# Layer 0's router and experts in one block, with GpSimd taking two of four groups' low parts

## The reference

```python
def _route(x, gate_w, gate_bias):            # 64 experts in 8 groups of 8
    scores = sigmoid(x @ gate_w.T)
    choice = scores + gate_bias
    # a group's score: its two best choices, summed; the best 4 groups are kept
    # of these the best 8 experts; their scores, divided by their sum, times 2.5
    ...
def _mlp(x, gw, uw, dw):
    return silu(x @ gw.T) * (x @ uw.T) @ dw.T  # inner width 88 for each expert
out = sum over experts of rw[:, e] * _mlp(x, Wg[e], Wu[e], Wd[e]) + _mlp(x, Sg, Su, Sd)
x = layernorm(x + out)                         # before it and after it: attention and layernorm
```

## Time and profile before

| | |
|---|---|
| median of 3 runs | 1407.01 us (1405.93 to 1410.32) |
| profiled execution | 1402.02 us, its span 1400.3 us |
| busy over the span | PE 91%, DVE 80%, ACT 64%, POOL 34% |
| mean granted clock of PE | 0.946 of full speed |

### The profile page before, as it was taken

The page is one execution under the profiler, slowest core; times in us unless marked ns, Lnnn a source line. Parts: engine busy times, 40 slices in busy tenths (PEclk is TensorE's granted clock), DMA queues, the critical chain, the costliest instruction groups (busy, mean ns, idle before and its releaser), DMA issues. The chain is left out here.

```text
span 1400.3 us, 21389 instructions
## 1 busy us (share of the span) xinstructions
PE 1279.3 (91%) x7374; PEld 711.9 (51%) x7374; DVE 1114.2 (80%) x1726; ACT 898.5 (64%) x1503; POOL 481.3 (34%) x988
## 2 busy tenths in 40 slices
PE   5898987169999999999889999999999998999998
PEld 2222224157777777777643232223222337777776
DVE  5677763758999999999758788888889747688886
ACT  4988873034555555555453788888888866767775
POOL 4565551014334343334142244224422422221210
PEclk8898988579999999999999999999999999999999
DMA  5422200064666666666236555434342201121200
GB/s 156 127 56 66 63 21 7 0 134 110 147 143 154 148 151 151 147 146 152 79 113 146 111 156 133 121 102 104 88 123 61 53 11 52 62 91 46 91 31 31
DMA packets 70020, 135.87 MB, mean 97 GB/s; under 512 B 13031, under 2 KB 44328, under 8 KB 63112
## 3 DMA queue, kind: packets, MB, share of 16 engines
q1 hardware_dynamic: 68760, 133.46, 37.5%
q10 hardware_dynamic: 1152, 1.05, 0.2%
HBM read 116.87 MB, written 16.29 MB: 95 GB/s over the span
## 5 line engine op out<-in xcount | busy, mean ns | idle before, releaser
L1589 ACT ACTIVATE a_PR<-n1a_C 128x512 f32<-128x512 f32 x576 | 299.6, 603 | 79.5 <-PE n1a_C L1495 79.4
L1604 DVE CUSTOM_DVE_ANT_0 OC_last<-a_mring,a_COR 128x1024 bf16<-128x1024 f32 x256 | 302.6, 1218 | 42.4 <-PE a_mring L1462 42.1
L1432 POOL TENSOR_SCALAR_AFFINE_SELECT a_PR<-a_PR 128x128 f32<-128x128 f32 x512 | 136.2, 296 | 250.2 <-ACT a_PR L1589 249.7
L868 ACT ACTIVATE e_HH<-e_H 128x512 fp32r<-128x512 f32 x184 | 116.4, 633 | 158.3 <-DVE e_H L916 157.5
L1495 PE MATMUL n1a_C<-a_QP,a_KP 74*128 74x512 bf16 (+3 forms) x768 | 176.1, 332 | 4.4 <-ACT a_PR L1589 3.5
L402 ACT ACTIVATE a_PR<-a_ring,a_ng 128x1024 f32<-128x1024 f32 (+1 forms) x160 | 150.2, 1045 | 26.0 <-PE a_ring L345 26.0
L427 DVE TENSOR_SCALAR a_PR<-a_PR,a_lo,a_hi 128x1024 f32<-128x1024 f32 (+1 forms) x160 | 119.2, 763 | 56.1 <-ACT a_PR L402 55.6
L1514 PE MATMUL n1a_C<-a_PR,a_V 128*9 128x512 f32 (+3 forms) x1536 | 152.1, 492 | 0.0
L887 DVE TENSOR_TENSOR e_HL<-e_H,e_HH 128x512 fp32r<-128x512 f32 x138 | 139.4, 1010 | 13.5 <-DVE e_H L904 0.5
L810 POOL TENSOR_TENSOR e_HL<-e_H,e_HH 128x512 fp32r<-128x512 f32 x46 | 78.5, 1706 | 180.5 <-ACT e_HH L868 180.5
L1883 DVE TENSOR_TENSOR e_HL<-e_GL,e_HH 128x512 fp32r<-128x512 f32 x144 | 109.5, 765 | 38.3 <-ACT e_HH L1851 34.7
(11 more groups left out here) (257 smaller groups left out, 2252.6 us busy)
## 6 DMA issues: line engine op xcount, KB each, us to landing
e_ROUTE<-routing SPq DMA_DIRECT2D x24, 704.0 KB
a_QP<-q_parts SPq DMA_DIRECT2D x72, 192.0 KB
e_RAW<-in_w_chunks SPq DMA_DIRECT2D x46, 192.0 KB, 7.4
a_QM<-q_parts SPq DMA_DIRECT2D x64, 128.0 KB, 2.8
e_GATE<-gates SPq DMA_DIRECT2D x8, 1024.0 KB, 4.4
e_ROUTE<-routing SPq DMA_DIRECT2D x8, 640.0 KB
a_KP<-k_parts SPq DMA_DIRECT2D x24, 192.0 KB
e_ROUTE<-routing SPq DMA_DIRECT2D x8, 576.0 KB
```

What stands on the lines that cost most here:

```text
L868: nc.scalar.activation(HH[n % NH][:], HT[n % NH][:], ACT.Copy).then_inc(high_done, 1)
L1432: last = nc.gpsimd.affine_select(out=d, in_=d, compare_op=keep, fill=0.0, base=0, pattern=[[step, P]], channel_multiplier=-step)
L1589: nc.scalar.activation(PR[:, g % NPR, j, :], ring[n % NRING][:], ACT.Exp).then_inc(s_read, 1)
L1604: nc.vector.tensor_tensor_reduce(out=junk[:, i % 2, :], in0=mring[k % 2][:], in1=COR[:, c:c + S], scale=1.0, scalar=-3.0e38, op0=ALU.mult, ...
```

## The change

`route_l0` and `experts_l0` become one block, `moe_l0`, and some of its work is done in the normalisation before it.

- In `normalise` ("n0a"): SP loads the router's weights and four chunks of expert weights; PE makes the logits of a group as soon as it is rescaled; ACT makes the high part of X and the scores; POOL makes both parts of three chunks' weights and the low part of X.
- In `moe_l0` DVE's routing instructions have the first 20 products of silu and up between them. The choice of the two best experts of a group is made with maxima and minima of halves. Hidden values of 24 steps are kept (`NTR`). The multiplication by the routing weight is 20 steps behind the product, the low part 21, the down product 23.
- The shared expert's down product is one float32 product with the weights in `RAW`, with no split.
- POOL makes the low part of every odd step, and the high part of the weights, six chunks ahead of the low parts that follow it. From chunk 8 on the weights' low part is on DVE. ACT copies the transposed routing weights.
- Weights have 8 buffers and 4 for the raw values, routing rows three as before.
- In `project_l1` the sixteen matmuls at the end become five, and five are added in front of the last but one group's product.

```diff
-def normalise(nc, name, X, consts, signals, turn, Y=None, update=None, C=None, out=None, load_ahead=None):
+def normalise(nc, name, X, consts, signals, turn, Y=None, update=None, C=None, out=None, load_ahead=None, ahead=None):
...
                     variance_of(g)
                     spread_inverse(g - 1)
+                    if ahead is not None and g >= 2:
+                        ahead.logits_of(pe, g - 2, done, base + g - 1, C[g - 2])
                 spread_inverse(NG - 1)
+                if ahead is not None:
+                    for g in range(NG - 2, NG):
+                        ahead.logits_of(pe, g, done, base + g + 1, C[g])
...
+                if ahead is not None:
+                    for g in range(NG - 2, NG):
+                        ahead.high_of_x(act, g, done, base + g + 1)
+                    for g in range(NG):
+                        ahead.scores_of(act, g, C[g])
+            if ahead is not None:
+                @block.gpsimd
+                def _(pool):
+                    for c in range(ahead.FIRST):
+                        ahead.split(pool, c)
+                    for g in range(NG):
+                        ahead.low_of_x(pool, g)
...
+    def load_chunk(self, sp, c):
+        if c >= NRAW:
+            self.await_low(sp, c - NRAW)
+        if NRAW <= c < NRAW + CHS:
+            sp.wait_ge(self.down_done, (c - NRAW + 1) * NG)
+        sp.dma_start(self.RAW[c % NRAW][:], self.a["w_chunks"][c]).then_inc(self.w_loaded[c % NRAW], 16)
+    def split(self, pool, c):
+        raw, high, low = self.RAW[c % NRAW], self.WH[c % NSLOT], self.WL[c % NSLOT]
+        pool.wait_ge(self.w_loaded[c % NRAW], (c // NRAW + 1) * 16)
+        if c >= NSLOT:
+            pool.wait_ge(self.down_done, (c - NSLOT + 1) * NG)
+        self.nc.gpsimd.tensor_copy(high[:], raw[:]).then_inc(self.w_high, 1)
+        if c < NSLOT:
+            pool.wait_ge(self.w_high, c + 1)
+            self.nc.gpsimd.tensor_tensor(low[:], raw[:], high[:].bitcast(F32), ALU.subtract).then_inc(self.w_low_pool, 1)
+    def split_low(self, dve, c):
+        raw, high, low = self.RAW[c % NRAW], self.WH[c % NSLOT], self.WL[c % NSLOT]
+        dve.wait_ge(self.w_high, c + 1)
+        self.nc.vector.tensor_tensor(low[:], raw[:], high[:].bitcast(F32), ALU.subtract).then_inc(self.w_low_dve, 1)
...
+            def _(sp):
+                for c in range(NRAW, 2 * NRAW):
+                    ahead.load_chunk(sp, c)
+                for g in range(NG):
+                    sp.wait_ge(kept, g + 1)
+                    sp.dma_start(routing[:, grp(g)], RT[:, grp(g)]).then_inc(stored, 16)
+                sp.wait_ge(stored, 16 * NG)
+                for c in range(CHS, CHS + NR):
+                    load_route(c)
+                for c in range(2 * NRAW, NCH):
+                    ahead.load_chunk(sp, c)
+                    if c - 2 * NRAW - 1 >= CHS + NR:
+                        load_route(c - 2 * NRAW - 1)
+                for c in range(NCH - 2 * NRAW - 1, NCH):
+                    load_route(c)
...
+            def _(pool):
+                for c in range(ahead.FIRST, NCH + POOL_BEHIND):
+                    if c < NCH:
+                        ahead.split(pool, c)
+                    if c - POOL_BEHIND >= CHS:
+                        for n in range((c - POOL_BEHIND) * NG, (c - POOL_BEHIND + 1) * NG):
+                            if on_pool(n):
+                                low(n)
...
+            def _(pe):
+                for n in range(N):
+                    if n == TURN:
+                        turn_weights()
...
+                    product(psG[n % 2], s, 0, g).then_inc(gate_ready, 1)
+                    product(psU[n % 2], s, 1, g).then_inc(up_ready, 1)
+                    if 3 <= n < NSH + 3:
+                        down_shared(n - 3)
+                    if n - DOWN >= NSH:
+                        down(n - DOWN)
...
+            def _(act):
+                for n in range(N + BEHIND + 1):
+                    if n == TURN:
+                        for g in range(NG):
+                            act.wait_ge(turned, g + 1)
+                            nc.scalar.activation(RT[:, grp(g)], banks[g][0:NE0, :], ACT.Copy).then_inc(kept, 1)
+                    if n < N:
+                        silu(n)
+                    if n - BEHIND - 1 >= NSH:
+                        high(n - BEHIND - 1)
...
+                for n in range(BEHIND + NSH, N + BEHIND + 1):
+                    if n < N:
+                        product(n)
+                    if n % NG == 0 and n // NG + 1 < NCH:
+                        ahead.split_low(dve, n // NG + 1)
+                    if n - BEHIND - 1 >= NSH:
+                        low(n - BEHIND - 1)
+                    if n - BEHIND < N:
+                        weigh(n - BEHIND)
...
-                        pe.wait_ge(cor_loaded, 32)
...
+                    if g == NG - 2:
+                        pe.wait_ge(cor_loaded, 32)
+                        keep_busy(psV, 5)
...
-                keep_busy(psQ[0], 16)
+                keep_busy(psQ[0], 5)
```

More of the change, by code:

```diff
@@ L727, in experts_l0, with moe_l0 @@
+def moe_l0(nc, X, Y, last_outputs, ahead, consts, routing, part):
+    NR = 3
     NH = 4
-    LAG = 3
+    TURN = 20
+    BEHIND = 20
+    DOWN = BEHIND + 3
+    NTR = 24
     NSH = CHS * NG
@@ new lines, in link @@
+                def link(ins, then=0):
+                    links[0] += 1
+                    ins.then_inc(step, 1)
+                    for _ in range(then):
+                        product(products[0])
+                        products[0] += 1
+                    dve.wait_ge(step, links[0])
+                by_group = ch.rearrange("p t (g e) -> p (t g) e", g=NGRP)
+                flat = lambda t: t[:].rearrange("p t g -> p (t g)")
+                wide = lambda t, k: flat(t).unsqueeze(2).to_broadcast([P, NT_TOK * NGRP, k])
@@ new lines, in _ @@
+                link(v.tensor_tensor(best[:], best[:], second[:], ALU.add), 1)
+                others = best[:].unsqueeze(2).to_broadcast([P, NT_TOK, NGRP, NGRP])
+                own = best[:].unsqueeze(3).to_broadcast([P, NT_TOK, NGRP, NGRP])
+                pair = t1.rearrange("p t (i j) -> p t i j", i=NGRP)
+                link(v.tensor_tensor(pair, others, own, ALU.is_ge), 1)
+                link(v.tensor_tensor(t1, t1, ahead.tri[:, 0:NGRP].rearrange("p i j -> p (i j)").unsqueeze(1)
+                                     .to_broadcast([P, NT_TOK, NE0]), ALU.mult), 1)
@@ new lines, in _ @@
+                for n in range(products[0], BEHIND + NSH):
+                    product(n)
+                for n in range(BEHIND + NSH, N + BEHIND + 1):
+                    if n < N:
+                        product(n)
+                    if n % NG == 0 and n // NG + 1 < NCH:
[4 more added lines that the diff above has]
+                        weigh(n - BEHIND)
@@ L1997, in build @@
         with ExitStack() as part:
-            Y = sbuf(nc, part)("Y_m0", [P, TOK], F32)
-            route_l0(nc, X, a["gate_w"], a["gate_bias"], a["earlier"], consts, routing0)
-            experts_l0(nc, X, Y, routing0, a["w_chunks"])
+            ahead0 = AheadMoeL0(nc, part, X, a)
+            normalise(nc, "n0a", X, consts, signals, 0, update=output0, load_ahead=ahead0.load, ahead=ahead0)
+            moe_l0(nc, X, OC, last, ahead0, consts, routing0, part)
             def load_ahead(sp):
```

396 lines of the change are left out of this document (179 added, 217 removed).

## The result

| | median | runs | against before |
|---|---|---|---|
| before | 1407.8 us | 4 runs, 1405.9 to 1410.3 | |
| after | 1429.28 us | 4 runs, 1424.8 to 1438.3 | 1.0159, 95% interval 1.0106 to 1.0213 |

The account below looks back on a forecast made before the run. It took PE and DVE as both near their limits, DVE with POOL slightly behind PE. The stage came to 465.4 us in place of 448.8, +16.6; with -2.0 for the projection, net +14.6 on 1407.0: 1421.6 us, range 1395 to 1441.

Parts of the forecast that it names:

- step 5: 38 steady chunks: DVE waits about 2.0 us for POOL's cast behind a low part; 9.22 us a chunk against 8.37, 350.4 together.
- step 2: Routing with 20 products between: DVE's list 38 us, PE hidden; with transposes and PE's next step, product 20 starts at 43.4.
- step 4: Behind product 28: DVE stands 15 us for chunk 8's weights, whose load SP issues behind seven DMAs of routing rows.
- The normalisation: Block before the experts: grows by 5.0 us through the last group's logits, high part, table load, sigmoids and X's low part.
- Steps 20 to 27: After routing: these steps are on PE, 8 x 1.36 = 10.9 us, so product 28 comes at 54.3.
- the first rival: Steady chunks: routing rows, not the cast, hold DVE; no chunk below 8.4 us; 1390.4 us in all; chance 0.14.
- The end: Behind the last products: 21 low parts and multiplications left, two steps 3.2 us, 37.3 us to the last matmuls.
- Layer 1's projection: Block behind the experts: with five matmuls at its end PE ends earlier and ACT is last: -2.0 us.
- That chunk 8 would not wait: Second rival, at chunk 8: weights pass the routing rows, so 15 us less, 1406.3 us, no change; chance 0.08.
- The clock fell: Rival: PE's clock falls, more likely only in the routing part and at chunk starts, +13 and +10: 1445 us; chance 0.10.
- DVE and POOL shut each other out: Expert chunks and end: instructions reading two SBUF tiles exclude each other; side by side would make 18 us less.

Follow-up runs that it names:

- raw_first: Changed kernel with the loads of the weights of chunks 8 to 11 issued before the store of the routing weights: 1419.94 us, ratio 1.0078.
- rows_early: Changed kernel with each chunk's routing rows issued in front of the weights' load that stood before them in SP's list: 1424.5 us, ratio 1.0140.
- proj_old: Changed kernel with layer 1's projection as before (sixteen matmuls at its end, none in front of the last but one group's product): 1432.37 us, ratio 1.0168.
- behind7: Changed kernel with POOL's cast of a chunk's weights one chunk's low parts further ahead (POOL_BEHIND 7 in place of 6): 1395.82 us, ratio 0.9918.
- three pairs: Kernels with new against old layer 1 projection, otherwise alike: the changed kernel, the kernel before, and a later faster candidate; -1, -1 and -5 us for the new one.
- combined: Changed kernel with the edits of behind7, raw_first and rows_early together: 1381.21 us, ratio 0.9800.
- pool_first: Changed kernel with only one of four low parts on POOL, that of step 4k + 1, POOL_BEHIND still 6: 1400.37 us, ratio 0.9932.

## Why the prediction was right, step by step

The sign, the place and the mechanism were right; the time was 7.7 us short, within the range. The stage took +24.4 where +16.6 was added up, so the shortfall lies in the stage, most of it in step 5. Two smaller errors went opposite ways (+3.3 in step 2, -1.5 in step 4) and partly cancelled.

1. *The normalisation*: +5.0 forecast, 244.86 - 240.44 = +4.4. Of this 0.8 had arisen before the normalisation (its first ACT instruction stands at 222.67, before at 221.88), so the block itself grew by 3.6.
2. *Routing and 20 products*: product 20 forecast at 43.4 after the block's start, measured 46.7. DVE's list was through at 40.5 (38 forecast), and product 20 came 6.2 later (5.4 forecast): PE made its matmuls at a granted clock of 0.54, in 2.7 us. The small instructions together took about 2.0 less than the sum, since one starts before the last has ended. What the sum lacked: one of the three reductions reads with a stride and took 2.11, not 1.23; the first two instructions were held up by POOL's subtraction (0.26 and 0.70); and DVE did wait for PE, four times, 2.5 us in all. The forecast held PE hidden at 1.36 for a step. In these steps it also does a down product of the shared expert (L850), and the clock is 1.00. DVE's product and PE in order of time:

```profile
262.97 0.69 DVE L924 TENSOR_TENSOR e_T<-e_SG,e_psU 128x512 f32<-128x512 f32 x1 [1.03 <-PE e_psU L835]
...
265.22 0.69 DVE L924 TENSOR_TENSOR e_T<-e_SG,e_psU 128x512 f32<-128x512 f32 x1 [0.43 <-PE e_psU L835]
```

```profile
258.26 1.02 PE L850 MATMUL e_acc<-e_T,e_RAW 128*128 128x512 f32 x2
258.72 0.80 PE L833 MATMUL e_psG<-e_XH,e_WH 128*128 128x512 f32 x1
259.36 0.40 PE L834 MATMUL e_psG<-e_XL,e_WH 128*128 128x512 f32 x1
...
260.50 1.02 PE L850 MATMUL e_acc<-e_T,e_RAW 128*128 128x512 f32 x2
```

   A step is 2.24 us so, and DVE asks for one each 1.9. The float32 product takes 0.87 (1.10 from its start to the second matmul behind it, less 0.23 for the first), more than the 0.68 (half of 1.36) of three fp32r matmuls. The forecast said in passing that these down products shrink by 2 us together; they grow, by 0.19 each, and in these steps it is what makes DVE wait.
3. *Steps 20 to 27*: 10.9 forecast, 10.9 measured (291.54 to 302.44).
4. *The new wait*: 15 forecast, 13.5 measured, at the place and by the load that were named. raw_first shows that its cause is the order in SP's list. DVE went on at 71.8, forecast 70.1.
5. *38 chunks*: 9.22 forecast, 9.16 to 9.2 by the cast alone (the chunk above, rows_early), 9.42 in fact. DVE's wait is 1.9 (2.03 forecast), PE's idle 0.7. The term that the forecast lacked is the mechanism of the first rival, which I had weighed only as an alternative: rows come late even at 9.2 a chunk, since their issue stands behind a load that waits. Over 37 distances this 0.2 is 7.4 us, nearly all of what the block took beyond the forecast (468.8 against 460.4); in `proj_old` it was about half of that. The order inside a chunk was as forecast too: the low part that POOL's other one shuts out ended 8.6 after the chunk's first product.
6. *The end*: 37.3 forecast, 36.5 measured, two steps 3.16 (3.2 forecast).
7. *Layer 1's projection*: -2.0 forecast; the block itself is 3.2 shorter (32.7 in place of 35.9), but in the profiled execution the attention behind it had a granted clock of 0.79 over its first 70 us, not 0.95, and took 14 us longer. By the three pairs what is left is -1 to -5, none of it beyond what a pair can tell, so this term is neither borne out nor refuted.

The +24.4 is of one execution and the +22 of the medians. They fit together if most of the 11.8 us behind the experts belong to that execution more than to the kernel; this isn't shown by itself, but the same code took between 659.9 and 672.7 us there in nine kernels, and 672.7 is this one.

On the rivals: the routing rows do not set the cycle, but add to it. The first rival's floor, no chunk below 8.4, does not hold either: behind7 has 8.34 and `combined` 8.26. That chunk 8 would not wait was wrong by 13.5 us (and its time, by the forecast's own 15 us, should read 1406.6, not 1406.3). The clock fell in three places, but not in the steady chunks (1.00 there): at the transposes (0.55 from 284 to 289), while PE stood at chunk 8 and for its first matmuls behind that (0.50 from 312 to 322), and in the attention. At chunk 8 it cost nothing that shows, since the first chunk behind it took 9.15 us, no more than the others.

DVE and POOL shut each other out as forecast: DVE's low part takes 0.69 alone and 1.25 beside POOL's. The Trainium skill ("SBUF — State Buffer", section "SBUF: two separate sides") calls this an exclusive lock, and the trace agrees. No run takes the lock away alone, so its price isn't measured. But it did not make the move a loss: behind7 has POOL's two low parts and the lock and is 0.8% faster than the kernel before, and both its chunk and its end are shorter than those of pool_first, with half as many low parts on POOL. From 0.69 to 1.25 in each of some ten pairs at the end is about 6 us by estimate, which is where it still weighs.

## What to carry over

When work moves to another engine, write down that engine's list and ask of each instruction that somebody else waits for (here a cast of 0.5 us) what stands in front of it and what that waits for; its place may cost more than the work moved: here it was worth 34 us of 1429. The same goes for the engine that issues DMAs: a small load needed soon (192 KB here) does not belong behind 3 MB needed later; that was worth 11 us. A distance that a pipeline needs at its start is paid at its end, in time in which the engine that sets the pace has little to do, unless it shrinks on the way.

## What the runs showed of the hardware

- One float32 product of 128x512 from weights of 128x128 took 0.87 us of PE at full clock, three fp32r matmuls of that shape 0.68, both read from the distances between starts (the rows at step 2 above).
- A reduction of 128x1024 elements by eights took 1.21 us reading in order and 2.11 us where its inner index had a stride of eight elements:

```profile
L982 DVE TENSOR_REDUCE r_below<-OC 128x128 f32<-128x1024 f32 x1 | 2.1, 2114 | 0.0
...
L981 DVE TENSOR_REDUCE r_ranks<-OC 128x128 f32<-128x1024 f32 x1 | 1.2, 1212 | 0.0
```

- The same stretch of code gets different clocks on PE. With the new projection, in the profiles of nine kernels that differ only in front of it (one profile each), the first 70 us of the attention had 0.79 to 0.95, and the time from its first matmul to the end spread over 12.8 us. With the old projection (three profiles) it was 0.90 to 0.95 and 658.5 to 661.3 us. What decides it stays open.
